# An audio tower on one core: TensorE's order inside a pair of weights, the latents' norm on another engine, and 64-wide middles for the experts

## The reference, cut to what matters

```python
# tokens: x (64, 5000), weight (16, 5000, 128), mask (5000, 128)
h = einsum('bg,egp->bep', x, weight * mask) + bias          # 64 x 16 tokens of 128
# attention over the 16 tokens of a row, causal, 8 heads of 16 + 2 rotary dimensions
n   = layernorm(h)
cq  = layernorm(n @ W_dq) * g_q + b_q      # 64 latents for the queries
ckv = layernorm(n @ W_dkv) * g_kv + b_kv   # 85 latents for keys and values
q, k, v = heads(cq @ W_uq, rope(cq @ W_qr)), heads(ckv @ W_ukv, rope(n @ W_kr)), ...
h = h + softmax(q k^T * scale) v @ W_o.T
# experts: 64 of them, 64 wide inside, two for each token, at most 256 pairs each
f = layernorm(h)
scores = sigmoid(f @ gate_w.T); top 2, normalised, times 2.5
routed = sum over both: weight * ((silu(f @ w1[e]) * (f @ w3[e])) @ w2[e])
shared = (silu(f @ sw1) * (f @ sw3)) @ sw2
h = h + shared + routed
```

## Time and profile before

| what | us |
|---|---|
| runs of before | 254.86, 255.87, 255.04 (median 255.04) |
| profiled execution: its own time | 254.33 |
| its span | 252.6 |
| PE busy | 179.7 (71%) |
| DVE busy | 168.4 (67%) |
| POOL busy | 149.3 (59%) |
| ACT busy | 78.3 (31%) |
| mean granted TensorE clock | 0.924 of full |

### The profile page before, as it was taken

How to read it: one execution, slowest core, us unless ns; L and a number is a source line. 1 busy time by engine, 2 the same in 40 slices (tenths; PEclk the granted TensorE clock), 3 DMA queues, 4 the chain that set the end, 5 groups by cost and what they waited for, 6 DMA issues and landing times.

```text
span 252.6 us, 5556 instructions
## 1 busy us (share of the span) xinstructions
PE 179.7 (71%) x2207; PEld 148.8 (59%) x2207; DVE 168.4 (67%) x439; ACT 78.3 (31%) x202; POOL 149.3 (59%) x119
## 2 busy tenths in 40 slices
PE   0067877396989799599399299678866866998810
PEld 0067766365968589479289178456654756767410
DVE  0034374948698879779879975899997449255391
ACT  2005200021322221221221123246777563435500
POOL 3336489278978867977967967701422552037670
PEclk9999999979999979899989769967998899999985
DMA  7999999999999999997999999497011228114432
GB/s 247 248 362 416 350 420 333 418 416 421 414 418 425 416 422 416 411 417 270 403 273 221 235 207 156 89 306 204 0 42 44 64 72 243 46 51 136 126 96 53
DMA packets 32979, 65.07 MB, mean 258 GB/s; under 512 B 2874, under 2 KB 25367, under 8 KB 32375
## 3 DMA queue, kind: packets, MB, share of 16 engines
q1 hardware_dynamic: 31416, 59.47, 71.1%
q10 hardware_dynamic: 576, 3.26, 3.1%
q0 software_dynamic: 960, 1.97, 2.8%
HBM read 56.96 MB, written 7.73 MB: 256 GB/s over the span
## 4 chain that ended last, share of the span: by engine, by line
PE 33%; DVE 19%; SPq 17%; DMA 13%; ACT 8%; issue 5%; POOL 2%; POOLq 1%; DVEq 0%
DMA ring<-in_L_tok_weight_dram 12%; PE bank L798 9%; SPq L342 6%; PE bank L959 5%; PE bank L986 4%; DVE ring L1171 4%; SPq L358 3%; DVE prod L1222 2%; DVE bank L1230 2%; ACT mask L666 2%; SPq L348 2%; POOL ring L516 2%; DVE bank L1204 2%; PE bank L937 2%; PE bank L943 1%
## 5 line engine op out<-in xcount | busy, mean ns | idle before, releaser
L446 POOL TENSOR_TENSOR ring<-ring,mask 128x896 f32<-128x896 f32 (+1 forms) x48 | 92.2, 1947 | 18.3 <-DMA ring<-in_L_tok_weight_dram 18.2
L798 PE MATMUL bank<-ring,xT 128*64 128x128 f32 x1248 | 84.2, 292 | 9.5 <-DVE ring L1171 6.4
L798 PEld LDWEIGHTS bank<-ring,xT 128*64 128x64 f32 x1248 | 74.7, 147 | 15.4 <-DVE ring L1171 7.7
L1171 DVE TENSOR_TENSOR ring<-ring,bank 128x1024 f32<-128x1024 f32 (+1 forms) x45 | 46.3, 1048 | 32.7 <-DMA ring<-in_L_tok_weight_dram 32.5
L435 POOL TENSOR_TENSOR rstd<-mv,half 128x1 f32<-128x1 f32 (+1 forms) x24 | 14.4, 602 | 39.3 <-DVE mv L1182 39.3
L516 POOL DMA_INDIRECT ring<-expert_outputs,gather_index x16 | 16.1, 1004 | 20.0 <-DMA expert_outputs<-ring 14.7
L986 PE MATMUL bank<-w2p,ring 128*128 128x128 f32 (+1 forms) x128 | 14.1, 290 | 5.8 <-ACT ring L674 3.5
L466 POOL DMA_INDIRECT expert_inputs<-xf,scatter_index x14 | 14.3, 1022 | 6.5 <-issue 3.3
L986 PEld LDWEIGHTS bank<-w2p,ring 128*128 128x128 f32 (+1 forms) x128 | 12.1, 172 | 8.2 <-ACT ring L674 7.5
L779 PE MATMUL bank<-cst,w 64*128 64x64 f32 x39 | 5.3, 328 | 15.7 <-DMA w<-in_x_dram 15.1
L561 ACT ACTIVATE offset<-shift,rstd 128x1 f32<-128x1 f32 x16 | 4.6, 290 | 37.3 <-POOL rstd L435 37.0
(11 more groups left out here) (147 smaller groups left out, 305.4 us busy)
## 6 DMA issues: line engine op xcount, KB each, us to landing
ring<-in_L_tok_weight_dram SPq DMA_DIRECT2D x48, 832.0 KB, 13.5
expert_inputs<-w ACTq DMA_DIRECT2D x3, 1024.0 KB, 10.1
ring<-expert_inputs SPq DMA_DIRECT2D x6, 512.0 KB, 5.4
expert_outputs<-ring SPq DMA_DIRECT2D x12, 256.0 KB, 2.5
mask<-in_L_tok_mask_dram SPq DMA_DIRECT2D x3, 832.0 KB, 15.8
w<-in_x_dram SPq DMA_DIRECT2D x1, 1250.0 KB, 13.2
w2p<-in_L_ffn_w_dram SPq DMA_DIRECT2D x1, 1024.0 KB, 19.3
xT<-masks_dram SPq DMA_DIRECT2D x1, 1024.0 KB, 8.0
```

Of the source, the lines that this page charges most:

```text
L446: pool.tensor_tensor(unit(j, q, SPLIT(q // 2), UC), unit(j, q, SPLIT(q // 2), UC), mask[:, (m + SPLIT(q // 2)) * D:(m + UC) * D], ALU.mult ...
L798: last = pe.matmul(bank[0][64 * par:64 * par + 64, 0:D], xT[:, (UC * t + c) * B:(UC * t + c + 1) * B], unit(j, 2 * t + par, c, c + 1), sta ...
L1171: dve.tensor_tensor(both(j, t, a, b), both(j, t, a, b), m.rearrange("p (u f) -> p u f", u=1).to_broadcast([P, 2, (b - a) * D]), ALU.mult). ...
```

## The change

TensorE sums quarters 0 and 1 of a pair ahead of `turn_o`; `attend` and `project` follow the turns at once; quarter 2 stands ahead of `turn_xf` and `turn_qk`, quarter 3 ahead of `gate` and `qkv`, quarter 4 ahead of the ranks and values. VectorE's pieces are dealt out 2, 2, 1, 1 over its turn, and the norm of the next h stands ahead of the choice of experts.

The latents' norm goes to ScalarE: the projections are centred once (`centre_projections`, so that the latents' mean is zero), ScalarE squares with a sum along the row (the bias gives epsilon), GpSimd takes the root as before, ScalarE scales. The slot of a token is made with one instruction less, and the gathers use the same index as the scatters.

The experts' middles are 64 wide. One plain copy replaces the two masked ones, the product is 128x256, `turn_mid` is eight 64x64 matmuls with the identity in place of four 128x128 transposes, `copy_midT` is 256 wide, and `down` is one matmul for each expert with 64 rows of the array. In round 2 a permuted copy of the gate's weights (`gwT2`) names the experts so that those of one parity lie in one half of the rows. Group 7's product is GpSimd's, and `turn_mid(7)` and `down(7)` stand ahead of round 2's first turns.

The diff, cut to its core:

```diff
-VECTOR_SHARE = (2, 1, 1, 1, 1)
+VECTOR_SHARE = (2, 2, 1, 1)
...
+def PLACE(g, n):
+
+    slots = EXPERTS(g)[2]
+    row, tile = n * slots % P, n * slots // P
+    return row, tile, row // H, row % H
+
+
+def EXPERT(g, n):
+
+    first, _, slots = EXPERTS(g)
+    return first + n if slots == SLOTS else first + n // 4 * 4 + n % 2 * 2 + n % 4 // 2
...
+    c[:, C_EPS] = math.sqrt(EPS / QP)
+    c[:, C_EPS + 1] = math.sqrt(EPS / KVP)
...
-                pool.tensor_tensor(hm[g % 2].rearrange("p i (a h) -> p i a h", a=2),
-                                   sil[g % 2].rearrange("p i (a h) -> p i a h", a=1).to_broadcast([P, PG, 2, H]),
-                                   gt[g % 2].rearrange("p i (a h) -> p i a h", a=2), ALU.mult).then_inc(s_hm, 1)
-
-            pool.wait_ge(s_held, 4)
-            pool.wait_ge(s_masked, 6)
+                pool.tensor_tensor(hm[g % 2], sil[g % 2], gt[g % 2], ALU.mult).then_inc(s_hm, 1)
...
+            def square_qk(j):
+                act.wait_ge(s_proj, j + 1)
+                if j >= 1:
+                    act.wait_ge(s_qkn, j)
+                for i, (a, n) in enumerate(((C_QKV, QP), (C_QKV + QP, KVP))):
+                    last = act.activation(sq_junk[:, i, 0:n], bank[3][:, a:a + n], ACT.Square, bias=cst[:, C_EPS + i:C_EPS + i + 1],
+                                          scale=1.0 / math.sqrt(n), accum_out=mv[:, 1 + i, 1:2])
+                last.then_inc(s_var_qk, 1)
+
+            def norm_qk(j):
+                act.wait_ge(s_rstd_qk, j + 1)
+                act.activation(qkn[:, 0:QP], bank[3][:, C_QKV:C_QKV + QP], ACT.Identity, scale=rstd[:, 1:2])
+                act.activation(qkn[:, QP:], bank[3][:, C_QKV + QP:C_QKV + QP + KVP], ACT.Identity, scale=rstd[:, 2:3]).then_inc(s_qkn, 1)
...
+                    act.copy(as_round_two(gwT2[:]), natural(bank[6][:, D:D + E])).then_inc(s_wT, 1)
...
-                if g < GROUPS1 - 1:
-                    for par in range(2):
-                        act.activation(gt[g % 2][:, :, H * par:H * par + H], both[:, :, H:2 * H], ACT.Identity,
-                                       scale=cst[:, C_PAR + par:C_PAR + par + 1])
+                if g < GROUPS1:
+                    act.copy(gt[g % 2], both[:, :, H:2 * H])
...
-                act.copy(hT[g % 2], bank[M_BANK(g)][:]).then_inc(s_hT, 1)
+                act.copy(hT[g % 2], bank[M_BANK(g)][:, 0:PG * H]).then_inc(s_hT, 1)
...
             keep_h(l)
+            square_qk(k)
             score_exp(0, NCH1)
+            norm_qk(k)
+            norm_h(l)
             turned_qk(k)
-            norm_h(l)
             heads_k(k)
             copy_oT(j)
             heads_v(k)
+            copy_xnT(l)
             copy_xsT(0)
-            copy_xnT(l)
+            square_qk(l)
             copy_xsT(1)
             probs(k)
+            norm_qk(l)
             silu(0)
             turned_qk(l)
             norm_xf(j)
...
+                    pe.wait_ge(s_centred, 2)
                 project_b, attend_d = b >= 0, d >= 0
+                sum_genes(c, 0)
+                sum_genes(c, 1)
                 if attend_d:
                     turn_o(d)
                 if project_b:
                     turn_xn(b)
-                sum_genes(c, 0)
                 if attend_d:
                     attend(d)
                 if project_b:
                     project(b)
-                for n in range(1, 4):
-                    sum_genes(c, n)
+                sum_genes(c, 2)
                 if attend_d:
                     turn_xf(d)
                 if project_b:
                     turn_qk(b)
-                sum_genes(c, 4)
+                sum_genes(c, 3)
                 if attend_d:
                     gate(d)
                 if project_b:
                     qkv(b)
+                sum_genes(c, 4)
                 if attend_d:
                     rank_tokens(d)
-                sum_genes(c, 5)
                 if project_b:
                     values(b)
-                for n in range(6, 12):
+                for n in range(5, 12):
...
-                    last = pe.transpose(bank[M_BANK(g)][:, i * P:(i + 1) * P], hm[MID_TILE(g)][:, i, :], ident)
+                    for par in range(2):
+                        rows = slice(H * par, H * par + H)
+                        last = pe.matmul(bank[M_BANK(g)][rows, i * H:(i + 1) * H], hm[g % 2][rows, i, :], ident[rows, rows],
+                                         start=True, stop=True)
...
-                for n in range(count // 2):
-                    row, tile = 2 * n * slots % P, 2 * n * slots // P
-                    last = pe.matmul(bank[Y_BANK(g)][row:row + 2 * slots, tile * D:(tile + 1) * D],
-                                     hT[g % 2][:, 2 * n * slots:2 * (n + 1) * slots], w2p[:, first // 2 + n, :],
-                                     start=True, stop=True)
+                for n in range(count):
+                    row, tile, par, col = PLACE(g, n)
+                    last = pe.matmul(bank[Y_BANK(g)][row:row + slots, tile * D:(tile + 1) * D],
+                                     hT[g % 2][H * par:H * par + H, tile * H + col:tile * H + col + slots],
...
+            turn_mid(7)
+            down(7)
             turn_xs(GROUPS1)
             add_last(GROUPS1)
-            turn_mid(7)
             turn_xs(GROUPS1 + 1)
             add_last(GROUPS1 + 1)
-            down(7)
             for g in range(GROUPS1, GROUPS + 2):
...
+            def centre_projections():
+
+                dve.wait_ge(s_pw, 64)
+                for i, (a, n) in enumerate(((0, QP), (QP, KVP))):
+                    mark(dve.tensor_reduce(mx[:, i, 0:1], wproj[:, a:a + n], AX.X, ALU.add))
                 marked()
-                aggregate(1, 3, s_var_qk)
-
-            def norm_qk(j):
-                dve.wait_ge(s_rstd_qk, j + 1)
-                norm(qkn[:, 0:QP], bank[3][:, C_QKV:C_QKV + QP], 1)
-                norm(qkn[:, QP:], bank[3][:, C_QKV + QP:C_QKV + QP + KVP], 2).then_inc(s_qkn, 1)
+                for i, n in enumerate((QP, KVP)):
+                    mark(dve.tensor_scalar(mx[:, i, 1:2], mx[:, i, 0:1], 1.0 / n, None, ALU.mult))
+                marked()
+                for i, (a, n) in enumerate(((0, QP), (QP, KVP))):
+                    dve.tensor_scalar(wproj[:, a:a + n], wproj[:, a:a + n], mx[:, i, 1:2], None, ALU.subtract).then_inc(s_centred, 1)
...
-                    mark(dve.tensor_scalar(slot[:, j, k:k + 1], topi[:, j, k:k + 1], slots, rank[:, k:k + 1], ALU.mult, ALU.add))
-                mark(dve.tensor_scalar(far(j), rank[:], slots, FAR, ALU.is_ge, ALU.mult))
+                where = s_idx[:, j, :] if j < NCH - 1 else last_slot[:]
+                mark(dve.scalar_tensor_tensor(spot[:, 0, :], topi[:, j, 0:2], slots, rank[:], ALU.mult, ALU.add))
+                mark(dve.tensor_scalar(spot[:, 1, :], rank[:], 0.5 - slots, FAR, ALU.add, ALU.mult))
                 marked()
-                where = s_idx[:, j, :] if j < NCH - 1 else last_slot[:]
-                dve.tensor_tensor(where, slot[:, j, :], far(j), ALU.add).then_inc(s_slot, 1)
+                dve.tensor_tensor(where, spot[:, 0, :], spot[:, 1, :], ALU.max).then_inc(s_slot, 1)
...
                 mask_pieces(VECTOR_SHARE[0])
                 if d >= 0:
                     add_attended(d)
-                if b >= 0:
-                    stats_qk(b)
                 if c == 1:
                     turn_rope()
-                mask_pieces(VECTOR_SHARE[1])
+                    centre_projections()
                 if c == 0:
                     dve.wait_ge(s_rem, 32)
                     dve.wait_ge(s_mrem, 16)
                     dve.tensor_tensor(wrem[0:GREM], wrem[0:GREM],
                                       mrem[0:GREM, :].rearrange("p (a n) -> p a n", a=1).to_broadcast([GREM, S, D]),
                                       ALU.mult).then_inc(s_remm, 1)
-                if b >= 0:
-                    norm_qk(b)
+                mask_pieces(VECTOR_SHARE[1])
+                if a >= 0:
+                    stats_h(a)
+                if d >= 0:
+                    choose(d)
                 mask_pieces(VECTOR_SHARE[2])
                 if d >= 0:
-                    choose(d)
-                mask_pieces(VECTOR_SHARE[3])
-                if d >= 0:
                     place(d)
-                if a >= 0:
-                    stats_h(a)
                 if b >= 0:
                     scores(b)
-                mask_pieces(VECTOR_SHARE[4])
-                if b >= 0:
                     less_max(b)
+                mask_pieces(VECTOR_SHARE[3])
                 if b >= 0 and c < NCH - 1:
                     heads(b)
             def shared_mid(i):
...
 
             def mid(g):
 
-                slots = EXPERTS(g)[2]
                 dve.wait_ge(s_sil, g + 1)
...
-                for r in range(P // slots):
-                    rows, half = slice(slots * r, slots * (r + 1)), r % 2 * H
```

(5 more changed lines are left out.)

115 lines of the change are left out of this document (53 added, 62 removed).

## The result

The changed kernel takes 266.63 us in the median of four executions (263.18 to 269.66) for 255.45 of the kernel before (254.86 to 257.10). Over the executions of either kernel that agree among themselves the ratio is 1.0382, interval 1.0265 to 1.0499. It is 4% slower; the forecast was 249.0 with a range of 245 to 257.5. The profiled execution took 263.18 us (span 261.4), 8.85 more than the 254.33 of the one before.

The account below looks back on a forecast made before the run. Weights' DMA was taken to bound up to 83 us, then the VectorE-TensorE ring to 161, later the experts' ring and TensorE. Terms -3.7 + 0.5 - 2.8 + 0.5 - 0.6 = -6.1 gave a 249.0 us median, range 245 to 257.5.

Parts of the forecast that it names:

- Part 1: The pairs: reordered TensorE work, latents' norm on ScalarE and shorter slots save 3.7 us, mostly 1.5 each in pairs 5 and 6.
- the sign of being wrong: In the pairs: GpSimd's roots starting only when its pieces let them, more than 4 us behind `o`.
- some 4 of exposed waits and clock: Pair 4: TensorE's turn, 13.5 us busy plus some 4, is about the old 17.9, so the gain is 0.5.
- a higher clock: In the pairs: less idle time before a pair leaves TensorE a higher clock; counted as nothing.
- One of six small instructions: The slots in a pair: VectorE loses one of six small instructions, 0.1 to 0.2 us.
- Rival 2: The pairs gain nothing: TensorE waits inside the pair and drops its clock, GpSimd answers later; -0.3 for -3.7, 252.4; chance 0.18.
- Rival 1: Experts' down matmuls and turns: row tiles writing one bank do not overlap, costing 10.6 us, 259.6; chance 0.20.
- Part 2: Behind the pairs: later latents' copies and a longer ScalarE queue against VectorE's saving, net +0.5 us, ends -1 and +2.
- Rival 3: ScalarE becomes the bound behind the pairs: +2 there and nothing from the experts' round 1, 253.3; chance 0.10.
- Parts 3 and 4: Experts: round 1's shorter ring -2.8 us, moving the last middle and down +0.5, round 2's single product -0.6.
- the squares and scalings: Latents' norm on ScalarE: two squares and two scalings at 0.4 us each, 1.6 a pair.
- scores at 10.1 and 10.6 behind `o`: Pairs 5 and 6: scores were to start 10.5 to 11 us from `o`.

Follow-up runs that it names:

- e12: e4 with 6 and 2 idle matmuls a pair (4 in pair 2) before the attended state's and latents' turns; 0.9936 of the kernel before.
- e13: Changed kernel, slots included, with 6 idle matmuls before the attended state's turn (8 before the latents' in pair 2); 0.9949 of the kernel before.
- e14: Changed kernel with old slots, idle matmuls at TensorE's waits and ScalarE's old order behind the pairs; ran 249.0, 252.2, 255.0 and 259.4 us.
- e15: e10 with 7, 7, 11 and 15 idle matmuls before the heads' turn in pairs 4 to 7; 0.9763 of the kernel before.
- e2: Changed kernel with the slots worked out as before the change; 1.0086 of the kernel before.
- e4: Kernel before with TensorE's new order of a pair alone; 1.0401 of the kernel before.
- e17: e15 with 9 idle matmuls before the turn of chunk 6's latents and 6 behind it; 0.9708 of the kernel before, median 249.8 us.
- e6: e5 with VectorE again norming the last two chunks' latents behind the pairs; 1.0124 of the kernel before.
- e10: e8 with ScalarE's norm of chunk 7's state put behind the scaling of chunk 6's turned latents; 0.9902 of the kernel before.
- e1: Kernel before with the experts' part of the change alone; 0.9993 of the kernel before.
- e3: Changed kernel with TensorE's order of a pair as before the change; 0.9872 of the kernel before.
- e8: Changed kernel with both TensorE's order and the slots as before the change; 0.9910 of the kernel before.
- e5: Changed kernel with TensorE's new order only in pairs 5, 6 and 7; 1.0127 of the kernel before.
- e11: e5 with the second of three slot instructions writing its result into PSUM; ran 253.35, 257.9, 261.2 and 263.7 us.

## Why the prediction was wrong

- **Part 1, the place of the loss.** I priced pairs 3 and 4 at gains of 0.2 and 0.5 us, by a count of latencies from `o`. They lost 6.3 and 0.8. In the early pairs `o` is there, or nearly, when the turn begins (TensorE waited 0.3 and 1.8 us for it in the pairs 3 and 4 before), so quarters put ahead of it do not fill a wait; they push the chain back. In pair 3 `turn_o` starts 2.4 us behind the end of `o`, and GpSimd's first root 4.8 us behind it for 3.1 before: beyond the 4 us that I had named as the sign of being wrong, though it waited for VectorE's variance, not for its own pieces. And the quarters are missed later, between the projection and the turns: 1.4 to 1.8 us a pair for the attended state. My own words were "some 4 of exposed waits and clock"; I used them as a limit to the gain and gave them no further price.
- **Part 1, the clock.** This is the step that failed: the -3.7 for the pairs holds no price for a lower clock behind new waits; "a higher clock ... I count nothing for it". I thought of the clock as a gain left out. It fell to 0.83, 0.85 and 0.82 in pairs 2, 3 and 4, from 0.95, 1.00 and 0.90 (pair 7's is as before). e12 puts what the idle gaps cost at 12 us when the order alone is changed, and e13 at 4% in the changed kernel; e14 against e15 shows that even the gain of pairs 5 and 6 (3.4 us measured for my 3.0), where the number was right, was the clock's and not the order's.
- **Part 1, the slots.** "One of six small instructions" was to save 0.1 to 0.2; the form behind it (128x2 with both sides in SBUF) cost up to 6.85 us an instruction, and e2 puts it at 3% of the changed kernel. I had read GpSimd's pieces and VectorE's slots in the same stretch and never asked what they share.
- **Rival 2** ("it has half the work between its waits for the norms, drops its clock there") is the mechanism that happened. I priced it as no gain (252.4), not as a loss. Its price, from e4 against e12, is 1.9, 1.5, 1.5, 1.4 and 3.0 us in the pairs 3 to 7, 9.4 in all, which by this estimate would have put it at 262.
- **Rival 1** is refuted by the tiles' times. Its number, 259.6, was the nearest, for the wrong reason.
- **Part 2** (+0.5): the first experts came 13.4 us behind the last pair's sums for 11.7, so +1.7, inside my ends. Two waits behind the pairs (2.26 and 1.66 us, for 2.43 and 0.89 before) were followed by the lower clock; e17 filled such waits and the 13.5 us stayed, so what makes the 1.7 is open. Rival 3's terms (+2, and nothing from part 3) are near what was measured; its cause, a ScalarE that bounds, is not borne out by e6 and e10.
- **Parts 3 and 4** (-2.8, +0.5, -0.6): the mechanism is right and the size is off. A turn lost 0.74 us, but only the last two turns count; the earlier ones end on the last `o` by VectorE, for which TensorE waits 2.40 us in both kernels. e1 measures the sum of both parts as 0.0 with 0.4% either way.
- Right: the squares and scalings (0.5 and 0.31 for 0.4 each), one product of 0.42 for 1.71, the copy of 0.37 to 0.40 for 0.38, scores at 10.1 and 10.6 behind `o`, the wait for `o` at 4.8.

Not settled: why the three mends (e2, e3, e13) each give back 3 to 5% though they act on different things. The causes are not independent: by the ratios the new order costs 1.8% with the old slots (e2 to e8) and 5.2% with the new ones (the changed kernel to e3), and the new slots cost 2.9% with the new order and nothing with the old. That a late VectorE lengthens TensorE's waits, and those lower the clock, would do it; no run isolates that loop.

## What to carry to other kernels

Work moved ahead of a wait is taken from another place: price the gap that it leaves, and price it with TensorE's lower clock over everything until the clock rises again. Where a gap can't be closed, idle matmuls cut to its length can be worth more than the reordering; cut too long they cost what they save. Before small VectorE instructions are widened or lose their PSUM operand, look at what GpSimd does beside them.

## What was not expected of the hardware

- VectorE's slot instructions of 128x2 with SBUF on both sides took 0.16 us alone and up to 6.85 us beside GpSimd's tensor_tensor (e5, e6, e11, e13, the changed kernel). Over all profiles, of those begun beside one of GpSimd's pieces none took under 0.39. The size matters as much as the place: 128x1 instructions with SBUF on both sides took 0.14 to 0.17 beside a piece in every profile, and 128x2 with one side in PSUM 0.15 to 0.16. So does the operation: a batch-norm aggregate of 128x2 took 0.18 there and a reciprocal of 128x8 0.20. The Trainium skill (SBUF — State Buffer, "Who interferes with whom") says that VectorE and GpSimd share a pair of ports as an exclusive lock for the whole instruction, which VectorE wants with two SBUF inputs or in its two-port modes. The trace agrees, and shows more: in pair 3 of the changed kernel each of the three instructions ended with one piece of GpSimd's, but in e5, e6 and e11 one instruction stood until three pieces in a row were done (6.17 us). What decides between the two is not shown.
- Idle matmuls alone changed the time by 12 us (e4 to e12).
- Matmuls on tiles that differ in rows and columns and write one PSUM bank overlapped: 16 records of 64x64 took 1.09 us, as long as 16 on column tiles. The Trainium skill (TensorEngine Tiling (Array Packing), "Gotcha 1: PSUM Pressure") says that different row tiles cannot access one bank at the same time; the measurement decides.
- A ScalarE activation that sums (`accum_out`) is followed by a read of the accumulator, 0.19 us each.
